# Cross-attention on one Trainium2 core: the weighted rows divided by their sums and the second norm on ScalarE, the weighted rows turned behind the weighting

## Chip, core and metric

The kernel runs on one core of a Trainium2 chip, as one program: TensorE (PE; its weight loads are shown apart, as PEld), VectorE (DVE), ScalarE (ACT), GpSimd (POOL) and SyncE (SP, which issues most of the transfers), each with its own list of instructions, held together by semaphores. The metric is the device time of one execution in microseconds (us). All data are fp32.

## What is computed

Three layers follow each other on 2048 rows (64 latents of 32 batches, 256 wide): a cross-attention to 1601 context rows of each batch, a grouped self-attention, and a mixture of experts. The change lies in the first:

```python
x = x + xattn(layernorm(x), ctx)                  # this change
x = x + attn(layernorm(x))
x = x + moe(layernorm(x))

def xattn(query, ctx):
    q = query @ Wq + bq; k = ctx @ Wk + bk; v = ctx @ Wv + bv
    probs = softmax(einsum('bqd,bkd->bqk', q, k))
    y = einsum('bqk,bkd->bqd', probs, v) + query
    return (y - mean(y)) * rsqrt(var(y) + 1e-5) * gamma + beta
```

The layernorm of its result, which the second layer starts from, is the "second norm" below. It is made in this stage too, and rows and normed rows leave together.

## The kernel before

**The pairs.** A pair is two batches, 128 rows. There are PAIRS = 16. The weights of queries and keys are multiplied beforehand and Wv is applied after the weighting, so that the raw context, in a ring of three slots in SBUF, serves as keys and as values. For pair i the steps are: `blocks_turned` (VectorE transposes the context in 8 column blocks, 5 of them early in a turn and 3 late), `scores` (TensorE, block by block, each behind its `block_ready`), `block_max` and `row_max` (VectorE), `exps` (ScalarE, which also sums), `row_sum` (VectorE, sum and its reciprocal `rinv`), `turn_probs` (TensorE turns the weights in four groups; the last group goes to the unused half of bank U), `turned_out` (ScalarE copies them to SBUF), `weigh` (TensorE, into U, 52 profiled records), `normalise` (U times `rinv` gives `Un`), `flip` (TensorE turns `Un`, in bank M), `UT_evac` (ScalarE copies it), `project` (TensorE, times Wv), `residual` (VectorE: adds the query row, first statistics, `scaled`), `first_norm` (VectorE: writes the new row to `stage[:, 0]`, second statistics), `deviation` (GpSimd: the power -1/2 of a variance), `second_norm` (writes `stage[:, 1]`), and `store` (SyncE sends `stage` to `mid` in DRAM).

**The turns.** The engines run through turns that are written by hand. In turn i TensorE does `scores(i)`, `flip(i-2)`, `weigh(i-1)`, `project(i-2)`, `turn_probs(i)`. VectorE does `block_max(i)`, `row_max(i)`, `second_norm(i-3)`, the 5 early blocks of pair i+1, `normalise(i-1)`, `row_sum(i)`, `residual(i-2)`, the 3 late blocks of pair i+1, `first_norm(i-2)`. ScalarE does `turned_out(i-1)`, `UT_evac(i-2)`, `exps(i)`. Turns 2 to 5 also hold work on queries (on VectorE `x_statistics` and `x_normed` in turn 3, `dots` in turns 2, 4 and 5), and ScalarE issues the stores of queries (`store_q`) behind turns 3 and 5. Turns 6 and up are hardware loops.

**Around the turns.** SyncE's `follow(i)` loads the queries of pair i, stores the rows of pair i-5 once `n1_ready` tells of their second norm, and then issues the ring loads of pair i, part by part behind `pv_done` of pair i-3. `flip` waits for `res_ready`, since it shares bank M with `project`. `first_norm(k)` waits until the rows of pair k-1 have been stored, because there is one `stage`.

**The end.** Behind turn 15 TensorE does `flip(14)`, the first part of `weigh(15)` (16 records), `project(14)`, the rest of `weigh(15)` (36 records), `flip(15)`, `project(15)`, some transposes of weights, and ten filler products (`keep_busy`, L1155), and then turns the first rows of the second layer (L1236), which are read back from `mid`.

## Time and profile before

| | us |
|---|---|
| median of three runs | 538.88 |
| lowest and highest | 538.51, 539.96 |
| the profiled execution, as timed | 540.22 |
| its span, first to last instruction | 538.5 |
| TensorE busy | 498.2 |
| VectorE busy | 399.3 |
| ScalarE busy | 200.1 |
| GpSimd busy | 198.0 |

The profiled execution lasts 1.7 us longer than its span, and 1.3 us longer than the median. Cross-attention takes the first 285 us or so of the span. The times in the rows are microseconds from the start of the span.

### The profile page before, as it was taken

The numbers are of one execution on the slowest core, as the hardware profiler recorded it, in microseconds if no ns is written. First come the engines' busy times: TensorE is split into PE (matmuls) and PEld (weight loads), VectorE is DVE, ScalarE is ACT, GpSimd is POOL, SyncE is SP. The second block draws the span as 40 slices with busy tenths as digits, with TensorE's granted clock in tenths as the row PEclk, the third lists the DMA queues.
The fourth block names the chain that finished last, engine by engine and source line by source line (L and its number), as shares of the span: only waits on it lengthen the run. The fifth ranks groups of instructions, "written<-read, shape, count | busy, mean of one in ns | idle before, by whom it ended". The sixth has DMA issues, their size and how long they took to land.

```text
span 538.5 us, 14453 instructions
## 1 busy us (share of the span) xinstructions
PE 498.2 (93%) x5012; PEld 348.7 (65%) x5013; DVE 399.3 (74%) x1068; ACT 200.1 (37%) x617; POOL 198.0 (37%) x314
## 2 busy tenths in 40 slices
PE   7988899999999999999989999999979899999950
PEld 7765566656666666666655667766735578888840
DVE  3699599999999999999653588888775325555545
ACT  2343323433223333333221366666341035555500
POOL 4000412212221112221222576766766616655620
PEclk9999999999999999999999999999998979999995
DMA  7999688877998888885215999710122245554249
GB/s 276 356 352 243 189 279 291 251 209 252 294 304 286 279 279 272 256 273 196 66 40 165 253 309 297 205 52 2 50 89 90 89 115 157 159 150 120 74 165 302
DMA packets 67348, 108.83 MB, mean 202 GB/s; under 512 B 8115, under 2 KB 49125, under 8 KB 67304
## 3 DMA queue, kind: packets, MB, share of 16 engines
q1 hardware_dynamic: 60888, 97.83, 58.6%
q0 software_dynamic: 3792, 8.43, 4.5%
q10 hardware_dynamic: 2624, 1.97, 1.2%
q8 instruction: 28, 0.46, 0.4%
q14 instruction: 16, 0.13, 0.1%
HBM read 85.31 MB, written 24.85 MB: 205 GB/s over the span
## 4 chain that ended last, share of the span: by engine, by line
PE 70%; DVE 9%; DMA 8%; POOL 5%; issue 4%; ACT 1%; SPq 1%; POOLq 0%; DVEq 0%; ACTq 0%
PE banks L1110 15%; PE banks L1134 15%; PE banks L1516 8%; DMA ring<-in_ctx_dram 5%; POOL rows_by_expert L727 4%; PE banks L1528 4%; PE banks L1122 3%; DVE ctxT L1638 3%; PE banks L1147 3%; PE banks L1069 2%; PE banks L1510 2%; DMA xn_all<-expert_out 2%; PE banks L1243 2%; PE banks L1295 2%; PE banks L1155 2%
## 5 line engine op out<-in xcount | busy, mean ns | idle before, releaser
L1638 DVE STREAM_TRANSPOSE ctxT<-ring 128x832 f32<-128x832 f32 x128 | 121.7, 1009 | 4.2 <-DMA ring<-in_ctx_dram 4.1
L1110 PE MATMUL banks<-ctxT,qT_all 32*64 32x416 f32 (+2 forms) x2048 | 93.9, 498 | 2.5 <-issue 2.1
L1134 PE MATMUL banks<-ring,prob 128*64 128x256 f32 (+1 forms) x832 | 93.6, 381 | 0.7 <-ACT prob L839 0.7
L1134 PEld LDWEIGHTS banks<-ring,prob 128*64 128x64 f32 (+1 forms) x832 | 58.6, 137 | 31.5 <-issue 4.2
L1110 PEld LDWEIGHTS banks<-ctxT,qT_all 32*64 32x64 f32 x2048 | 56.8, 131 | 31.2 <-issue 14.0
L638 POOL TENSOR_TENSOR var<-mv,eps 128x1 f32<-128x1 f32 x32 | 6.3, 196 | 168.6 <-DVE mv L1683 116.5
L761 POOL DMA_INDIRECT expert_out<-prob,dest x47 | 46.2, 984 | 41.6 <-DVE prob L2099 27.7
L852 ACT ACTIVATE prob<-banks,negmax 128x416 f32<-128x416 f32 (+2 forms) x80 | 41.1, 531 | 30.2 <-DVE negmax L1660 30.2
L1516 PE MATMUL banks<-ring,ctxT 128*128 x188 | 50.7, 394 | 0.1
L674 POOL TENSOR_TENSOR ctxT<-ctxT,k_mask 128x1088 f32<-128x1088 f32 x16 | 33.1, 2069 | 25.3 <-ACT ctxT L930 25.3
L839 ACT COPY prob<-banks 128x512 f32<-128x512 f32 x64 | 27.7, 514 | 38.0 <-PE banks L1122 37.9
L2092 DVE TENSOR_TENSOR ctxT<-banks,ctxT 128x128 f32<-128x128 f32 x47 | 13.7, 292 | 36.2 <-ACT ctxT L991 36.2
L1650 DVE TENSOR_REDUCE blockmax<-banks 128x1 f32<-128x416 f32 (+1 forms) x64 | 32.3, 567 | 10.2 <-PE banks L1110 10.2
L1516 PEld LDWEIGHTS banks<-ring,ctxT 128*128 128x128 f32 x188 | 33.3, 197 | 3.4 <-issue 0.5
L856 ACT COPY UT<-banks 128x256 f32<-128x256 f32 x16 | 6.0, 375 | 63.7 <-PE banks L1141 63.7
L1528 PE MATMUL banks<-ring,ctxT 128*128 x94 | 28.0, 381 | 0.0
L1122 PE MATMUL banks<-ident,prob 128*128 128x128 f32 (+1 forms) x208 | 26.1, 274 | 1.7 <-DVE Un L1672 0.9
L1122 PEld LDWEIGHTS banks<-ident,prob 128*128 128x128 f32 (+1 forms) x208 | 23.7, 140 | 4.8 <-ACT w_mem L804 1.6
L2099 DVE TENSOR_SCALAR prob<-banks,share 128x256 f32<-128x256 f32 x47 | 22.6, 481 | 2.7 <-PE banks L1528 0.8
L991 ACT ACTIVATE ctxT<-banks 128x128 f32<-128x128 f32 x47 | 13.0, 278 | 24.0 <-PE banks L1516 24.0
L1510 PE MATMUL banks<-ident,ctxT 128*128 128x128 f32 x94 | 18.9, 286 | 2.9 <-DMA ctxT<-rows_by_expert 2.9
L628 POOL TENSOR_SCALAR x_var<-x_mv 128x4 f32<-128x4 f32 (+1 forms) x5 | 1.3, 258 | 53.6 <-DVE x_mv L1587 53.6
(269 smaller groups left out, 940.5 us busy)
## 6 DMA issues: line engine op xcount, KB each, us to landing
ring<-in_ctx_dram SPq DMA_DIRECT2D x48, 1024.0 KB
qT_all<-q_by_pair SPq DMA_DIRECT2D x56, 128.0 KB, 8.9
rows_by_expert<-blank SPq DMA_DIRECT2D x8, 774.0 KB, 7.2
ctxT<-rows_by_expert SPq DMA_DIRECT2D x47, 129.0 KB, 2.1
mid<-stage SPq DMA_DIRECT2D x31, 128.0 KB, 2.3
ring<-in_ctx_dram SPq DMA_DIRECT2D x16, 130.0 KB
ctxT<-mid SPq DMA_DIRECT2D x16, 128.0 KB, 4.5
qT_all<-mid SPq DMA_DIRECT2D x16, 128.0 KB, 4.9
```

The costliest lines, as they stand in the source:

```text
L674: pool.tensor_tensor(k_blk, k_T.unsqueeze(2).broadcast_to([P, GB, HEADS, NP]), k_mask[:, :].unsqueeze(1).unsqueeze(3).broadcast_to([P, GB, ...
L761: pool.indirect_dma_start(y_dram, bass.IndirectOffsetOnAxis(ap=dest[:, s:s + 1], axis=0), y_sb[:, r, :], None, bounds_check=TOPK * TOK - 1 ...
L839: act.copy(probT[0:rows, ks[0]:ks[-1] + 1, :].rearrange("p a b -> p (a b)"), PT_BANKS[g][0:rows, 0:len(ks) * P]).then_inc(probT_copied, 1)
L852: act.activation(to, of, ACT.Exp, bias=negmax[:, 0:1], accum_out=sums[:, n:n + 1]).then_inc(exp_done, 1)
L1110: last = pe.matmul(S[a][64 * b:64 * b + 64, 0:KW[a]], q_rep[mine, r, c, 64 * b:64 * b + 64], ctxT[mine, c, b, 0:KW[a]], start=c == 0, stop ...
L1122: last = pe.transpose(PT_BANKS[g][0:rows, a * P:a * P + P], prob[:, k * P:k * P + rows], ident[:, :])
L1134: last = pe.matmul(U[64 * b:64 * b + 64, 0:D], probT[0:rows, k, 64 * b:64 * b + 64], ring[0:rows, r, b, k, :], start=k == 0, stop=k == KT)
L1510: last = pe.transpose(bank[r % 2][:, dh * P:dh * P + P], row_in[:, r, dh * P:dh * P + P], ident[:, :])
L1516: last = pe.matmul(bank[2 + p][:, 0:2 * HID], rowT[:, p, k, :], w_gu[:, bass.ds(e, 1), k, :].squeeze(1), start=k == 0, stop=k == DH - 1)
L1528: pe.matmul(bank[6 + p][:, 0:D], hidT[:, p, :], w_down[:, bass.ds(e, 1), :].squeeze(1), start=True, stop=True)\
L1638: dve.transpose(ctxT[:, c].rearrange("p b (k j) -> p (b k) j", j=Q), ring[:, r].rearrange("p b k c -> p (b k) c")[:, :, columns(c):columns ...
L1650: dve.tensor_reduce(blockmax[:, a:a + 1], S[a][:, 0:KW[a]], AX.X, ALU.max).then_inc(blockmax_ready, 1)
```

## The change

`normalise` moves from VectorE to ScalarE, behind `exps(i)`, as an activation with a scale of each row; since there is one `Un`, it now waits until `flip` of the pair before is through (`UT_done`), and VectorE's reciprocal waits until the last `normalise` has read `rinv`. `second_norm(i-3)` moves to ScalarE too, ahead of `exps(i)`, as scale and bias; the bias, minus mean times deviation, is made by GpSimd with two more instructions in `deviation(k, 1)`. The second norm of the last pair stays on VectorE. `UT_evac` goes behind `exps` and `normalise`. On TensorE `flip(i-2)` goes behind `weigh(i-1)`, and `project(i-2)` behind `turn_probs(i)`. The lines behind turn 15 on TensorE are not edited.

```diff
@@ -636,8 +636,15 @@
 
                 pool.wait_ge(mv_ready, 2 * k + (n + 1))
                 pool.tensor_tensor(var[:, n:n + 1], mv[:, n, 1:2], eps[:, :], ALU.add).then_inc(var_ready, 1)
-                pool.wait_ge(var_ready, 2 * k + (n + 1))
-                pool.tensor_tensor(rstd[:, n:n + 1], var[:, n:n + 1], m_half[:, 0:1], ALU.pow).then_inc(rstd_ready, 1)
+                if n == 0:
+                    pool.wait_ge(var_ready, 4 * k + 1)
+                    pool.tensor_tensor(rstd[:, 0:1], var[:, 0:1], m_half[:, 0:1], ALU.pow).then_inc(rstd_ready, 1)
+                else:
+                    pool.tensor_tensor(nmean[:, 1:2], mv[:, 1, 0:1], minus[:, :], ALU.mult).then_inc(var_ready, 1)
+                    pool.wait_ge(var_ready, 4 * k + 3)
+                    pool.tensor_tensor(rstd[:, 1:2], var[:, 1:2], m_half[:, 0:1], ALU.pow).then_inc(var_ready, 1)
+                    pool.wait_ge(var_ready, 4 * k + 4)
+                    pool.tensor_tensor(nmr[:, 1:2], nmean[:, 1:2], rstd[:, 1:2], ALU.mult).then_inc(rstd_ready, 1)
 
             def add_vectors(i):
 
@@ -851,11 +858,26 @@
                         to, of = by_slab[:, lo // Q, a, 0:hi - lo], S[a][:, lo:hi]
                     act.activation(to, of, ACT.Exp, bias=negmax[:, 0:1], accum_out=sums[:, n:n + 1]).then_inc(exp_done, 1)
 
+            def normalise(k, first=False):
+
+                act.wait_ge(pv_done, (k + 1) * len(KPARTS))
+                act.wait_ge(rinv_ready, k + 1)
+                if not first:
+                    act.wait_ge(UT_done, k)
+                act.activation(Un[:, :], U[:, 0:D], ACT.Copy, scale=rinv[:, 0:1]).then_inc(Un_ready, 1)
+
+            def second_norm(k):
+
+                act.wait_ge(rstd_ready, 2 * k + 2)
+                act.activation(stage[:, 1, :].rearrange("p (h v) -> p v h", h=HEADS),
+                               stage[:, 0, :].rearrange("p (v h) -> p v h", h=HEADS), ACT.Identity, bias=nmr[:, 1:2],
+                               scale=rstd[:, 1:2]).then_inc(n1_ready, 1)
+
             def UT_evac(i):
                 act.wait_ge(UT_done, i + 1)
                 act.copy(UT[:, :, :].rearrange("p a b -> p (a b)"), M[:, 0:D]).then_inc(UT_copied, 1)
 
-            def turn(i, ahead=True, back1=True, back2=True, rows=None, queries=None):
+            def turn(i, ahead=True, back1=True, back2=True, back3=True, rows=None, queries=None):
 
                 if back1:
                     turned_out(i - 1)
@@ -863,19 +885,25 @@
                     rows_turned(rows)
                 if queries:
                     query_blocks(queries)
+                if back3:
+                    second_norm(i - 3)
+                if ahead:
+                    exps(i)
+                    normalise(i - 1)
                 if back2:
                     UT_evac(i - 2)
-                if ahead:
-                    exps(i)
+                if back1 and not ahead:
+                    normalise(i - 1)
 
             exps(0)
             query_blocks(0)
             turned_out(0)
             exps(1)
+            normalise(0, first=True)
             rows_turned(1)
             query_blocks(1)
             store_q(1)
-            turn(2, rows=2)
+            turn(2, back3=False, rows=2)
             turn(3, queries=2)
             store_q(2)
             turn(4, rows=3)
@@ -1165,21 +1193,21 @@
                     queries_turned(rows)
                 if queries:
                     queries_of(queries)
+                if back1:
+                    pe.wait_ge(Un_ready, i - 1)
+                    weigh(i - 1, (r - 1) % RING)
                 if back2:
                     if back3:
                         pe.wait_ge(res_ready, i - 2)
                     flip(i - 2)
-                if back1:
-                    pe.wait_ge(Un_ready, i - 1)
-                    weigh(i - 1, (r - 1) % RING)
-                if back2:
-                    project(i - 2)
                 if rows:
                     pe.wait_ge(xnT_copied, 2 * rows + 4)
                 if queries:
                     pe.wait_ge(qT_copied, 2 * queries + 2)
                 if ahead:
                     turn_probs(i)
+                if back2:
+                    project(i - 2)
 
             pe.wait_ge(bk_row_copied, 1)
             scores(0, 0, 0, True)
@@ -1659,17 +1687,13 @@
                 dve.wait_ge(topped_ready, i + 1)
                 dve.tensor_tensor(negmax[:, :], shift[:, bass.ds(i, 1)], topped[:, :], ALU.subtract).then_inc(negmax_ready, 1)
 
-            def row_sum(k):
+            def row_sum(k, first=False):
                 dve.wait_ge(exp_done, (k + 1) * len(EXPS))
                 dve.tensor_reduce(rowsum[:, :], sums[:, :], AX.X, ALU.add).then_inc(rowsum_ready, 1)
                 dve.wait_ge(rowsum_ready, k + 1)
+                if not first:
+                    dve.wait_ge(Un_ready, k)
                 dve.reciprocal(rinv[:, :], rowsum[:, :]).then_inc(rinv_ready, 1)
-
-            def normalise(k):
-
-                dve.wait_ge(pv_done, (k + 1) * len(KPARTS))
-                dve.wait_ge(rinv_ready, k + 1)
-                dve.tensor_scalar(Un[:, :], U[:, 0:D], rinv[:, 0:1], None, ALU.mult).then_inc(Un_ready, 1)
 
             def residual(k):
 
@@ -1712,22 +1736,18 @@
                                              scalar=bk_row[:, D:D + 1], op0=ALU.mult, op1=ALU.add,
                                              accum_out=shift[:, a:a + 1]).then_inc(dot_ready, 1)
 
-            def turn(i, r, round_, ahead=True, more=True, back1=True, back2=True, back3=True, also=(), of_x=None):
+            def turn(i, r, round_, ahead=True, more=True, back2=True, also=(), of_x=None):
 
 
                 if ahead:
                     block_max(i)
                     row_max(i)
-                if back3:
-                    second_norm(i - 3)
                 if more:
                     blocks_turned(i + 1, (r + 1) % RING, round_ + (1 if r == RING - 1 else 0), range(0, EARLY))
                 if also:
                     dots(*also)
                 if of_x:
                     x_statistics(of_x)
-                if back1:
-                    normalise(i - 1)
                 if ahead:
                     row_sum(i)
                 if back2:
@@ -1750,13 +1770,12 @@
             blocks_turned(1, 1, 0, range(BLOCKS))
             dots(1, 3)
             x_statistics(2)
-            row_sum(0)
+            row_sum(0, first=True)
 
             block_max(1)
             row_max(1)
             x_normed(2)
             blocks_turned(2, 2, 0, range(EARLY))
-            normalise(0)
             row_sum(1)
             blocks_turned(2, 2, 0, range(EARLY, BLOCKS))
             dots(3, 4)
@@ -1764,7 +1783,7 @@
             x_normed(3)
 
             dve.wait_ge(rest_loaded, 112)
-            turn(2, 2, 0, back3=False, also=(4, 6))
+            turn(2, 2, 0, also=(4, 6))
             turn(3, 0, 1, of_x=4)
             turn(4, 1, 1, also=(6, 9))
             turn(5, 2, 1, also=(9, PAIRS))
@@ -1772,11 +1791,8 @@
                 for u in range(RING):
                     turn(it * RING + u, u, it)
             turn(PAIRS - 1, (PAIRS - 1) % RING, PAIRS // RING, more=False)
-            second_norm(PAIRS - 3)
             residual(PAIRS - 2)
             first_norm(PAIRS - 2)
-            normalise(PAIRS - 1)
-            second_norm(PAIRS - 2)
             dve.wait_ge(prep_loaded, 16 * (GB + 6))
             dve.tensor_copy(w_qp[:, :].rearrange("p (h v) -> p h v", h=HEADS), w_q.rearrange("p (v h) -> p h v", h=HEADS))\
                 .then_inc(w_qp_ready, 1)
```

TensorE in a turn of the loop, before; `Un` is what `flip` turns, `prob` what `turn_probs` turns, `UT` and `wv` are `project`, `ring` is `weigh`:

```order
L1110 MATMUL banks<-ctxT,qT_all 64x384 x2
L1141 MATMUL banks<-ident,Un 128x128 [waits Un_ready,res_ready]
L1141 MATMUL banks<-ident,Un 128x128
L1127 REGISTER_ALU [waits Un_ready]
L1134 MATMUL banks<-ring,prob 64x256 [waits probT_copied]
L1134 MATMUL banks<-ring,prob 64x256 x25
L1147 MATMUL banks<-wv,UT 128x256 [waits UT_copied]
L1147 MATMUL banks<-wv,UT 128x256
L1116 ISA
L1122 MATMUL banks<-ident,prob 128x128 [waits exp_done]
L1122 MATMUL banks<-ident,prob 128x128 x11
L1122 MATMUL banks<-ident,prob 65x128 [waits Un_ready]
```

The same place now:

```order
L1138 MATMUL banks<-ctxT,qT_all 64x384 x2
L1155 REGISTER_ALU [waits Un_ready]
L1162 MATMUL banks<-ring,prob 64x256 [waits probT_copied]
L1162 MATMUL banks<-ring,prob 64x256 x25
L1169 MATMUL banks<-ident,Un 128x128 [waits Un_ready,res_ready]
L1169 MATMUL banks<-ident,Un 128x128
L1144 ISA
L1150 MATMUL banks<-ident,prob 128x128 [waits exp_done]
L1150 MATMUL banks<-ident,prob 128x128 x11
L1150 MATMUL banks<-ident,prob 65x128 [waits Un_ready]
L1175 MATMUL banks<-wv,UT 128x256 [waits UT_copied]
L1175 MATMUL banks<-wv,UT 128x256
```

The two turns of `Un` stand behind the weighting, and the projection behind the turned weights, as the last thing ahead of the next scores.

ScalarE at the end of cross-attention (the copies of the last turned weights, then `UT_evac(14)` and `UT_evac(15)` in one row, then copies of turned weights of later layers), before:

```order
L839 COPY prob<-banks 128x512 [waits probT_done] x3
L839 COPY prob<-banks 65x128 [waits probT_done]
L856 COPY UT<-banks 128x256 [waits UT_done] x2
L890 COPY turned<-banks 128x512 [waits prep_done] x4
L892 DMA mid<-stage 64x512 [waits n1_ready]
```

The same place now:

```order
L846 COPY prob<-banks 128x512 [waits probT_done] x3
L846 COPY prob<-banks 65x128 [waits probT_done]
L872 ACTIVATE stage<-stage,nmr,rstd 128x16x16 [waits rstd_ready]
L878 COPY UT<-banks 128x256 [waits UT_done]
L867 ACTIVATE Un<-banks,rinv 128x256 [waits UT_done,rinv_ready,pv_done]
L872 ACTIVATE stage<-stage,nmr,rstd 128x16x16 [waits rstd_ready]
L878 COPY UT<-banks 128x256 [waits UT_done]
L918 COPY turned<-banks 128x512 [waits prep_done] x4
```

Each `UT_evac` now stands behind a second norm: that of pair 14 behind the norm of pair 13, that of pair 15 behind the norm of pair 14.

TensorE at the end, now (before, L1147 for pair 13 stood ahead of L1122, and the rest was the same):

```order
L1150 MATMUL banks<-ident,prob 65x128 [waits Un_ready]
L1175 MATMUL banks<-wv,UT 128x256 [waits UT_copied]
L1175 MATMUL banks<-wv,UT 128x256
L1169 MATMUL banks<-ident,Un 128x128 [waits Un_ready,res_ready]
L1169 MATMUL banks<-ident,Un 128x128
L1162 MATMUL banks<-ring,prob 64x256 [waits probT_copied,Un_ready]
L1162 MATMUL banks<-ring,prob 64x256 x7
L1175 MATMUL banks<-wv,UT 128x256 [waits UT_copied]
```

`project(13)` now stands right ahead of `flip(14)`, which waits for the `residual` that reads it; the last row, `project(14)`, has the other 18 instructions of `weigh(15)` queued behind it.

## Rows read from the trace of the kernel before

**Rows 1.** The page: busy us, share of the span, instructions, by engine.

```profile
PE 498.2 (93%) x5012; PEld 348.7 (65%) x5013; DVE 399.3 (74%) x1068; ACT 200.1 (37%) x617; POOL 198.0 (37%) x314
```

**Rows 2.** Timeline of TensorE in turn 10: start, length, line, names [idle before <-releaser].

```profile
188.39 5.83 PE L1134 MATMUL banks<-ring,prob 128*64 128x256 f32 x52
194.15 1.13 PE L1147 MATMUL banks<-wv,UT 128*128 128x256 f32 x4
195.12 1.58 PE L1122 MATMUL banks<-ident,prob 128*128 128x128 f32 x13
196.63 5.82 PE L1110 MATMUL banks<-ctxT,qT_all 32*64 32x416 f32 x128
202.38 0.44 PE L1141 MATMUL banks<-ident,Un 128*128 128x128 f32 x2
202.74 0.44 PE L1134 MATMUL banks<-ring,prob 128*64 128x256 f32 x2
```

**Rows 3.** Timeline of VectorE in the same turn.

```profile
190.82 0.51 DVE L1703 TENSOR_SCALAR stage<-stage,mv,rstd 128x256 f32<-128x256 f32 x1
...
196.58 0.43 DVE L1678 TENSOR_TENSOR res<-banks,xn_all 128x256 f32<-128x256 f32 x1
...
198.21 2.88 DVE L1638 STREAM_TRANSPOSE ctxT<-ring 128x832 f32<-128x832 f32 x3
...
202.58 0.59 DVE L1650 TENSOR_REDUCE blockmax<-banks 128x1 f32<-128x416 f32 x1 [0.39 <-PE banks L1110]
```

**Rows 4.** Timeline of weight loads: the last block of the scores of pair 10.

```profile
186.91 0.46 PEld L1110 LDWEIGHTS banks<-ctxT,qT_all 32*64 32x64 f32 x16 [0.24 <-DVE ctxT L1638]
```

**Rows 5.** Waits from 60 to 285 us: us in total, times, longest.

```profile
PEld banks L1122 <- DVE Un L1672: 1.6, 3, 0.7
```

**Rows 6.** Timelines of VectorE and of weight loads in turn 3.

```profile
88.50 0.42 DVE L1678 TENSOR_TENSOR res<-banks,xn_all 128x256 f32<-128x256 f32 x1 [0.30 <-PE banks L1147]
...
91.39 2.89 DVE L1638 STREAM_TRANSPOSE ctxT<-ring 128x832 f32<-128x832 f32 x3
...
94.37 0.21 PEld L1110 LDWEIGHTS banks<-ctxT,qT_all 32*64 32x64 f32 x12 [0.17 <-issue]
```

**Rows 7.** Timeline of all engines behind turn 15.

```profile
267.84 0.42 DVE L1678 TENSOR_TENSOR res<-banks,xn_all 128x256 f32<-128x256 f32 x1 [0.30 <-PE banks L1147]
...
270.14 1.95 PE L1134 MATMUL banks<-ring,prob 128*64 128x256 f32 x16 [0.69 <-ACT prob L839]
...
272.02 1.13 PE L1147 MATMUL banks<-wv,UT 128*128 128x256 f32 x4
272.22 0.50 DVE L1703 TENSOR_SCALAR stage<-stage,mv,rstd 128x256 f32<-128x256 f32 x1 [0.93 <-POOL rstd L640]
...
278.31 0.37 ACT L856 COPY UT<-banks 128x256 f32<-128x256 f32 x1 [8.04 <-PE banks L1141]
...
278.73 1.13 PE L1147 MATMUL banks<-wv,UT 128*128 128x256 f32 x4 [0.46 <-ACT UT L856]
```

**Rows 8.** Timeline of GpSimd in the second layer: first and last of the four-step deviation.

```profile
311.47 0.19 POOL L687 TENSOR_TENSOR var<-mv,eps 128x1 f32<-128x1 f32 x1
...
312.52 0.19 POOL L692 TENSOR_TENSOR nmr<-nmean,rstd 128x1 f32<-128x1 f32 x1
```

**Rows 9.** A ScalarE line with scale and bias: duration in ns (min/median/max), first and last start.

```profile
L903 ACT ACTIVATE ctxT<-x_all,nmr,rstd x12: 588/600/602, 312.7 to 374.3; 128x256 f32<-128x256 f32 x6, 128x256 f32 x6
```

**Rows 10.** Timelines of TensorE: its first work behind two long idle times of later layers.

```profile
403.00 1.20 PE L1410 MATMUL banks<-ring,turned 128*128 128x512 f32 x2 [2.05 <-DVE ctxT L2012]
...
432.00 1.09 PE L1510 MATMUL banks<-ident,ctxT 128*128 128x128 f32 x4 [2.94 <-DMA ctxT<-rows_by_expert]
```

**Rows 11.** Windows: busy share (count) of PE, PEld, DVE, ACT, POOL; granted clock, DMA, GB/s.

```profile
404.00:405.00 1.00, 1.00 (x3) 0.48 (x2) 0.00 (x0) 0.23 (x1) 0.78 (x1) 0.50 0.00 0
...
407.00:408.00 1.00, 1.00 (x3) 0.38 (x2) 0.00 (x0) 0.00 (x0) 0.73 (x1) 0.83 0.37 132
...
432.00:433.00 1.00, 1.00 (x4) 0.64 (x4) 0.32 (x4) 0.30 (x1) 0.00 (x0) 0.50 0.80 231
```

## The prediction, made before the changed kernel was run

> **What bounds the kernel now.** I read the page first: TensorE is busy for 498.2 us, 93% of the span, VectorE for 74%, ScalarE for 37% [rows 1]. Then a turn of the loop on TensorE [rows 2]. From start to start, the weighting takes 194.15 - 188.39 = 5.76 us, the projection 0.97, the turned weights 196.63 - 195.12 = 1.51, the scores 5.75, the flip 0.36. The sum, 14.35, is the whole turn (202.74 - 188.39): TensorE stands still nowhere. VectorE is nearly as full: it waits 0.39 us for the last scores [rows 3], and its last late block comes so late that the weight load of the eighth block of scores waited 0.24 us for it [rows 4]; TensorE's products themselves did not stop. So what the change takes off VectorE can only pay where TensorE waits for VectorE. That is one row of the waits: 1.6 us in 3 places, where the last group of turned weights waited for `Un` [rows 5].
>
> **Work taken away and added, in a turn.** VectorE loses the second norm (0.51 us, [rows 3]) and the division, which I take at the same size. ScalarE gets both. The nearest row has scale and bias and takes 0.60 us [rows 9]; a plain copy of the same size takes 0.37 [rows 7]. I take 0.6 for the norm, 0.5 for the division. ScalarE is idle for over half of the time [rows 1]; the norm stands where it would wait for the maxima, and the division where it would wait for the end of the weighting, so I cost both at nothing in the loop: the weighting's 5.76 us and the turned weights' 1.51 hide them. If that cover went, it would be 1.1 us a turn.
>
> The Trainium skill speaks against this move: "ScalarE: Activation LUTs", Rules for kernel authors, wants adds and multiplies on VectorE. What ACT_TABLE_LOAD costs, on the same page, gives 186 ns plus 0.833 ns per element plus 93 ns for each operand of a row, by estimate 0.59 us for the norm; the 0.60 of this trace agrees [rows 9]. By it the sum below stays as it is.
>
> **The removed waits: -1.6 us.** The division now runs right behind the weighting and the flip: flip, 0.4 for its landing, 0.5, while 12 of the 13 groups of turned weights (1.4 us) are still ahead of the one that waits. So the three waits go [rows 5]. Their bounds are 0 and 1.6; I take 1.6.
>
> **The later projection: +0.6 us in the loop, +1.5 us in turn 3.** The projection moves behind the turned weights, so it starts 1.51 us later in the turn. VectorE's `residual` reads it and stands ahead of the three late blocks. In the loop the projection would start at 195.66 and end, at 1.13 us, at 196.79; the residual started at 196.58 and now can't before 196.83, 0.25 us later. So VectorE's saved 1 us turns into waiting for TensorE, and the late blocks end 0.25 us later than before. The last weight load had no slack [rows 4]: it moves by about 0.2 us. What reaches TensorE lies between 0 (the loads run ahead of the products, and the flip between two other kinds of turning may shed some of its 0.36) and 0.2. I take 0.07 for each of nine turns (5 to 15, without the two behind a loop's end), 0.6 us; the bounds are 0 and 1.8.
>
> In turn 3 VectorE does more, and the residual already waited 0.30 us for the projection [rows 6]. Everything behind it is a chain: residual at 88.50, late blocks from 91.39 to 94.28, and the eighth block's weight load at 94.37, directly behind [rows 6]. The projection 1.51 us later moves all of it: +1.5. VectorE's saving ahead of the residual doesn't help, because the residual waits. ScalarE's `store_q` behind turns 3 and 5 now queues behind the late `UT_evac`, and `turned_out` behind that; in turn 3 the same 1.5 us cover it, in turn 5 it may cost a few tenths, which I leave to the range.
>
> **The end: +3.2 us.** This is the largest term. Here `project(13)` is behind the turned weights of pair 15, and there are no scores to cover anything.
> - `residual(13)` started at 267.84 [rows 7]; it moves by the turned weights less their overlap, 1.4 us, to 269.3.
> - From it to the end of GpSimd's deviation took 272.22 - 267.84 = 4.38 us [rows 7]. GpSimd now does two more small steps: the four take 312.71 - 311.47 = 1.24 us [rows 8], 0.4 over the two. So the second norm of pair 13 can start at 274.1 and takes 0.6 on ScalarE.
> - `UT_evac(14)` stands behind it. It starts at 274.6, and the projection followed such a copy by 278.73 - 278.31 = 0.42 us [rows 7]: `project(14)` at 275.0. Before, it was at 272.02 [rows 7]. That is +3.0 us. Behind it wait the 36 remaining records of `weigh(15)`, and all that follows.
> - `UT_evac(15)` stands behind the second norm of pair 14 in the same way. Residual at 275.0 + 1.2, then 4.4 + 0.4 + 0.6, gives 281.5 for the copy and 281.9 for `project(15)`, against 278.73 [rows 7]: +3.2 us in all. The fillers and the next layer stand behind it on TensorE, and the rows of pair 15 leave even later, so nothing takes it back. The bounds are 2.4 (norm at 0.37, no extra steps) and 4.
>
> **The clock: +1.3 us.** Between the first part of `weigh(15)` and `project(14)` TensorE now idles for 275.0 - 272.0 = 3 us. The trace has two idle times of 2 us or more ahead of product work: 2.05 and 2.94 us [rows 10]. Behind both the granted clock was 0.50, the 1.2 GHz level; the first time from 404 into the window from 407, over 3 us [rows 11]. Work at half rate for 3.3 us loses 1.7 us; part of it may fall into idle time. I take 1.3, with 0 and 3.3 (twice as long) as the bounds.
>
> **Sum.** -1.6 + 0.6 + 1.5 + 3.2 + 1.3 = +5.0 us. On the profiled execution, 540.2, that is 545.2. It lay 1.3 us above the median of the three runs, so the median should be 538.9 + 5.0 = **543.9 us**.
>
> **Rivals.**
> - The clock holds: the same without the last term, 538.9 + 3.7 = 542.6. For it: one place, with transposes and products on both sides; the two cases of the trace are few.
> - VectorE is the true bound of the loop, and the kernel gets faster. For it: the weight load that waited [rows 4], and 1 us less work a turn. If each of the 13 turns gave back only 0.7 us, that is -9.1; with the end, 538.9 - 9.1 + 4.5 = 534.3. It decides if the projection, once TensorE's turn shrinks, comes earlier than VectorE asks for it. Against it: the pieces of TensorE's turn fill it without a gap [rows 2]; no order of them is shorter.
> - The end doesn't stall: if `UT_evac(14)` finds the norm of pair 13 finished, the change does in sum +0.5, 539.4. For that the chain of 4.4 us behind the residual would have to hide behind a first part of `weigh(15)` of 1.9 us [rows 7]. It can't, unless later layers absorb the delay.
> - The transfers are late: the stores of queries go out 6 us later, and the load of pair 8 queues behind them; +1.5 more, 545.4. The second norm is earlier on ScalarE by a microsecond, and that helps the loads, since SyncE stores rows ahead of them.
>
> **How the numbers follow.** Forecast (clock falls) 0.45, clock holds 0.30, late transfers 0.09, faster 0.06, no stall 0.10. The first three lie between 541.2 (-1.6 + 0 + 1.5 + 2.4 + 0: no loss in the loop, the short end, the clock held) and 546.3 (-1.6 + 1.8 + 1.5 + 4 + 1.7). That holds 8 in 10, so the range is 541.2 to 546.3. A measurement can tell about 0.3%, 1.6 us, from no change: slower means above 540.5. Slower 0.84, the same 0.10, faster 0.06.
>
> **What would show it.** The turn in the loop stays between 14.35 and 14.6 us on TensorE, and VectorE waits for `project` ahead of each residual. The last turned group waits for `Un` nowhere. The scores of pair 4 end 1.5 us later. Behind turn 15 TensorE idles for 3 us ahead of `project(14)`, released by the copy of `UT`, which waited for the norm; and the windows behind it show a clock of 0.50, or not. I am wrong if the turn is shorter than 14.2 us, if that idle time is under 1 us, or if the second layer starts less than 2 us later.

## The result, and the profile after

| us | before | changed |
|---|---|---|
| median of 20 executions each, taken in turns | 539.46 | 541.14 |
| lowest and highest | 537.08, 542.31 | 537.60, 543.99 |
| the profiled execution, as timed | 540.22 | 541.16 |
| its span | 538.5 | 539.4 |

The changed kernel is slower: the ratio of the medians is 1.0046, with a 95% interval of 1.0031 to 1.0061, some 2.5 us. A second series on another occasion (below) gave 1.0057 [1.0035, 1.0079]. The forecast was +5.0 us and 543.9. The sign was right and the size twice too large: on the median that the forecast started from, the ratio gives 538.88 x 1.0046 = 541.4, just inside the low end of the range (541.2). The plain median, 541.14, lies just under it.

The page of the changed kernel, busy time by engine:

```profile
PE 497.0 (92%) x5012; PEld 344.0 (64%) x5013; DVE 391.6 (73%) x1037; ACT 216.7 (40%) x648; POOL 203.4 (38%) x346
```

Beside [rows 1], VectorE lost 7.7 us and ScalarE gained 16.6. The two steps were 14.9 us of VectorE's records; part of the difference is one small step, `topped`, which grew by 3.7 us in sum (below). The groups (line, operation, names and shapes, count; busy us and mean ns; idle time before them, and what ended it) show what the two moved steps cost. First VectorE before, the second norm and the division:

```profile
L1703 DVE TENSOR_SCALAR stage<-stage,mv,rstd 128x256 f32<-128x256 f32 x16 | 8.1, 505 | 2.0 <-POOL rstd L640 2.0
...
L1672 DVE TENSOR_SCALAR Un<-banks,rinv 128x256 f32<-128x256 f32 x15 | 6.9, 458 | 3.7 <-PE banks L1134 3.7
```

Then ScalarE in the changed kernel, the norm and the division:

```profile
L872 ACT ACTIVATE stage<-stage,nmr,rstd 128x256 f32<-128x256 f32 x15 | 12.4, 823 | 74.5 <-POOL nmr L647 74.5
L867 ACT ACTIVATE Un<-banks,rinv 128x256 f32<-128x256 f32 x15 | 7.1, 475 | 17.0 <-PE banks L1169 11.7 <-PE banks L1162 5.3
```

The division costs the same on both, 0.46 and 0.48 us. The norm takes 0.82 us instead of 0.51, and not the 0.6 that I read off [rows 9]. The idle time ahead of it, 74.5 us, stands ahead of `exps` and `UT_evac` too, since all are in one list.

**A turn of the loop.** Turn i is counted from the start of the scores of pair i to the start of those of pair i+1. Timeline of TensorE at the end of turn 11 and the start of turn 12 of the changed kernel (start, length, line, names); L1162 is the weighting, L1169 the flip, L1150 the turned weights, L1175 the projection, L1138 the scores:

```profile
207.23 0.44 PE L1169 MATMUL banks<-ident,Un 128*128 128x128 f32 x2
207.57 1.64 PE L1150 MATMUL banks<-ident,prob 128*128 128x128 f32 x13
209.04 1.03 PE L1175 MATMUL banks<-wv,UT 128*128 128x256 f32 x4
210.00 5.82 PE L1138 MATMUL banks<-ctxT,qT_all 32*64 32x416 f32 x128
215.75 5.83 PE L1162 MATMUL banks<-ring,prob 128*64 128x256 f32 x52
```

Against [rows 2] the flip takes 0.34 from start to start (before 0.36), the turned weights 1.47 (1.51), the projection 0.96 (0.97). Turn 11 is 14.28 us, against the 14.35 of [rows 2]. The nine turns from the start of the scores of pair 6 to that of pair 15 took 254.80 - 123.66 = 131.14 us before, and take 252.88 - 124.59 = 128.29 now: **2.85 us less**. The forecast had 1.0 less for the whole loop.

The last block of scores did become later, as forecast. Timeline of the weight loads of the same scores (those of pair 11, which start at 195.72):

```profile
200.60 0.24 PEld L1138 LDWEIGHTS banks<-ctxT,qT_all 32*64 32x64 f32 x16 [0.49 <-DVE ctxT L1666]
201.46 1.49 PEld L1162 LDWEIGHTS banks<-ring,prob 128*64 128x64 f32 x16 [0.62 <-issue]
```

Its first load stands 4.88 us behind the start of the scores; in turn 6, where it did not wait, it stands at 4.48. The first product of the block slips too, from 4.61 to 4.92. And yet the weighting's first load comes at 5.74, as it does anyway (from 196.63 to 202.38 in [rows 2], the flip there, it was 5.75): the slip is gone before the block ends. What is next is another chain. In turn 12 the last of `exps` ends at 221.80, and the turned weights start at 221.85. In turns 9 to 14 they follow `exps` by 0.05 us, so the maxima on VectorE and the exponentials on ScalarE now set these turns.

Part of that chain is new. Timelines of GpSimd and VectorE, in turn 10 before and in turn 11 of the changed kernel; `topped` is a step of `row_max`, `x_all` one of GpSimd's own additions:

```profile
189.50 0.73 POOL L647 TENSOR_TENSOR x_all<-x_all,beta_b 128x256 f32 x1
190.55 0.16 DVE L1658 TENSOR_TENSOR topped<-rowmax,shift 128x1 f32<-128x1 f32 x1
```

```profile
203.89 0.73 POOL L654 TENSOR_TENSOR x_all<-x_all,beta_b 128x256 f32 x1
204.00 0.63 DVE L1686 TENSOR_TENSOR topped<-rowmax,shift 128x1 f32<-128x1 f32 x1
```

Before, and in e4 below, every `topped` takes 0.16 us. In the changed kernel GpSimd's addition comes later and runs when `topped` starts in turns 4, 5 and 7 to 15, and each of these ends 0.01 to 0.02 us behind the addition, after 0.22 to 0.72 us. In turns 6 to 8, where `exps` still ends by 11.65 us into the turn, the turn is 14.17 us; in turns 9 to 14 `exps` ends at 11.80 to 11.84, and the turn is 14.28 to 14.32. That `topped` waits for GpSimd is read off these ends; no run moves the addition alone.

**Turns 3 and 5.** Both became longer, 18.33 us (17.84 before) and 18.59 (17.97). At the end of turn 5 TensorE shows a wait that was not there, and one of 0.46 us at the end of turn 3. TensorE and ScalarE (ACTq is its issuing of transfers, L820 is `store_q`):

```profile
121.75 0.33 ACTq L820 DMA_DIRECT2D q_by_pair<-w_mem  x1
122.07 0.36 ACT L878 COPY UT<-banks 128x256 f32<-128x256 f32 x1
122.11 1.43 ACTq L820 DMA_DIRECT2D q_by_pair<-w_mem  x3
123.75 1.72 ACT L846 COPY prob<-banks 128x512 f32<-128x512 f32 x4 [1.31 <-PE banks L1150]
...
124.59 2.84 PE L1138 MATMUL banks<-ctxT,qT_all 32*64 32x416 f32 x60 [0.72 <-ACT prob L846]
```

`turned_out` (L846) empties the banks that the next scores write. It queues behind four stores, 1.8 us of issuing. Before, the four were issued from 115.89 on, while `exps` still ran.

**The end.** Timeline of TensorE and ScalarE behind turn 15, which answers to [rows 7]:

```profile
268.12 1.95 PE L1162 MATMUL banks<-ring,prob 128*64 128x256 f32 x16
...
272.04 0.81 ACT L872 ACTIVATE stage<-stage,nmr,rstd 128x256 f32<-128x256 f32 x1 [4.74 <-POOL nmr L647]
272.67 0.40 ACT L878 COPY UT<-banks 128x256 f32<-128x256 f32 x1
273.12 1.13 PE L1175 MATMUL banks<-wv,UT 128*128 128x256 f32 x4 [3.05 <-ACT UT L878]
274.18 4.11 PE L1162 MATMUL banks<-ring,prob 128*64 128x256 f32 x36
...
280.18 1.13 PE L1175 MATMUL banks<-wv,UT 128*128 128x256 f32 x4 [0.81 <-ACT UT L878]
...
292.38 0.38 PE L1264 MATMUL banks<-ident,ctxT 128*128 128x128 f32 x2
```

This is what the prediction described: 3.05 us of idle TensorE ahead of `project(14)`, released by the copy of `UT`, which stood behind the norm, which waited for GpSimd. From the end of the scores of pair 15 to `project(15)` it was 278.73 - 260.61 = 18.12 us, and it is 280.18 - 258.70 = 21.48: **+3.36 us** (forecast +3.2).

In these two profiles the granted clock stayed at 1.00 through the end. Windows of the changed kernel (busy us with counts of PE, PEld, DVE, ACT, POOL; then the granted clock, DMA share, GB/s):

```profile
270.00:272.00 2.00, 0.07 (x2) 0.00 (x0) 0.66 (x3) 0.00 (x0) 1.07 (x4) 1.00 0.00 0
272.00:274.00 2.00, 0.89 (x4) 0.68 (x4) 0.00 (x0) 1.03 (x2) 0.00 (x1) 1.00 0.02 5
```

**The account.** Between the ends of the scores of pairs 2 and 15 the changed kernel needs 1.92 us less (196.14 against 198.06), from there to the first row of the second layer (L1264) 3.36 more (33.68 against 30.32). In sum the second layer starts 1.4 us later (292.38 against 290.94). The span ends 0.9 us later, since what is left of it took 247.0 us instead of 247.6. In that part the lead of 0.8 us comes between 416 and 445 us, where the granted clock was at 0.50 for 6.8 us in the profile before (from 431.2) and for 3.4 us in this one (from 435.5); the change has no instruction there.

### The profile page after: what moved, and what is told of

Its sections match the earlier page's. It is cut to its first block, busy times and chain, and to the rows that moved or that the text cites. A ratio compares the mean times of both kernels' runs of the same rounds, so it can differ in the third digit from the quotient of the medians.

```text
span 539.4 us, 14541 instructions
## 1 busy us (share of the span) xinstructions
PE 497.0 (92%) x5012; PEld 344.0 (64%) x5013; DVE 391.6 (73%) x1037; ACT 216.7 (40%) x648; POOL 203.4 (38%) x346
## 3 DMA queue, kind: packets, MB, share of 16 engines
q10 hardware_dynamic: 2624, 1.97, 1.1%
## 4 chain that ended last, share of the span: by engine, by line
PE 52%; issue 20%; POOL 10%; DVE 7%; DMA 6%; ACT 1%; SPq 1%; POOLq 1%; ACTq 0%; DVEq 0%
PE banks L1544 8%; PE banks L1138 8%; PE banks L1162 7%; POOL rows_by_expert L734 4%; PE banks L1556 4%; PE banks L1097 3%; DMA ring<-in_ctx_dram 2%; PE banks L1538 2%; DVE ctxT L1666 2%; DMA xn_all<-expert_out 2%; PE banks L1271 2%; PE banks L1150 2%; PE banks L1323 2%; PE banks L1183 2%; PE banks L1278 2%
## 5 line engine op out<-in xcount | busy, mean ns | idle before, releaser
L1138 PE MATMUL banks<-ctxT,qT_all 32*64 32x416 f32 (+2 forms) x2048 | 93.6, 500 | 2.2 <-ACT prob L846 1.2
L1162 PE MATMUL banks<-ring,prob 128*64 128x256 f32 (+1 forms) x832 | 93.6, 381 | 0.0
L1162 PEld LDWEIGHTS banks<-ring,prob 128*64 128x64 f32 (+1 forms) x832 | 58.3, 137 | 36.8 <-issue 9.3
L1138 PEld LDWEIGHTS banks<-ctxT,qT_all 32*64 32x64 f32 x2048 | 53.2, 131 | 36.6 <-DVE ctxT L1666 10.7
L872 ACT ACTIVATE stage<-stage,nmr,rstd 128x256 f32<-128x256 f32 x15 | 12.4, 823 | 74.5 <-POOL nmr L647 74.5
L846 ACT COPY prob<-banks 128x512 f32<-128x512 f32 x64 | 27.5, 525 | 6.1 <-PE banks L1150 6.1
L1150 PE MATMUL banks<-ident,prob 128*128 128x128 f32 (+1 forms) x208 | 25.8, 275 | 0.8 <-ACT w_mem L811 0.8
L1150 PEld LDWEIGHTS banks<-ident,prob 128*128 128x128 f32 (+1 forms) x208 | 22.7, 140 | 2.6 <-ACT w_mem L811 1.6
```

The source lines that it names most:

```text
L846: act.copy(probT[0:rows, ks[0]:ks[-1] + 1, :].rearrange("p a b -> p (a b)"), PT_BANKS[g][0:rows, 0:len(ks) * P]).then_inc(probT_copied, 1)
L1138: last = pe.matmul(S[a][64 * b:64 * b + 64, 0:KW[a]], q_rep[mine, r, c, 64 * b:64 * b + 64], ctxT[mine, c, b, 0:KW[a]], start=c == 0, stop ...
L1150: last = pe.transpose(PT_BANKS[g][0:rows, a * P:a * P + P], prob[:, k * P:k * P + rows], ident[:, :])
L1162: last = pe.matmul(U[64 * b:64 * b + 64, 0:D], probT[0:rows, k, 64 * b:64 * b + 64], ring[0:rows, r, b, k, :], start=k == 0, stop=k == KT)
```

## The experiments

Each was timed in turns with the kernel before (medians of 538.96 to 539.46 in the four series), and its ratio is to that. The counts are small: 20 executions of the changed kernel, 12 each of e1 to e4, 8 of e10, 7 of the changed kernel again, 6 each of e7 and e9, 4 of e6 and 2 of e5. The columns behind the ratio are from one profile each. "Loop" is the time from the end of the scores of pair 2 to the end of those of pair 15, "end" from there to `project(15)`, "second layer" from there to the first turned row of the second layer:

| kernel | median, us | ratio, interval | loop | end | second layer |
|---|---|---|---|---|---|
| before | 539.46 | 1 | 198.06 | 18.12 | 30.32 |
| changed | 541.14 | 1.0046 [1.0031, 1.0061] | 196.14 | 21.48 | 33.68 |
| changed again | 542.64 | 1.0057 [1.0035, 1.0079] | 196.15 | 22.79 | 35.00 |
| e1 ScalarE's end in another order | 539.94 | 1.0014 [0.9990, 1.0038] | 196.20 | 18.04 | 32.15 |
| e2 e1, and stores earlier | 538.60 | 0.9993 [0.9977, 1.0010] | 195.33 | 18.05 | 32.22 |
| e3 late blocks first | 541.76 | 1.0035 [1.0006, 1.0064] | 196.32 | 23.90 | 36.11 |
| e4 ScalarE's part alone | 538.20 | 0.9986 [0.9969, 1.0004] | 196.21 | 18.11 | 30.81 |
| e5 TensorE's part alone | 554.03 | 1.0271 [1.0254, 1.0289] | 207.86 | 18.97 | 34.07 |
| e6 six fillers | 544.87 | 1.0104 [1.0087, 1.0121] | 196.15 | 23.55 | 38.89 |
| e7 both orders mixed | 536.16 | 0.9946 [0.9932, 0.9961] | 194.33 | 18.13 | 30.70 |
| e9 three fillers | 544.43 | 1.0098 [1.0065, 1.0130] | 196.18 | 21.52 | 36.85 |
| e10 old order in turn 15 | 541.52 | 1.0052 [1.0030, 1.0074] | 196.70 | 20.18 | 35.51 |

**e1: is the end one queue?** The changed kernel, with ScalarE's last steps in another order:

```diff
-            turn(PAIRS, ahead=False)
-            turn(PAIRS + 1, ahead=False, back1=False)
+            turned_out(PAIRS - 1)
+            UT_evac(PAIRS - 2)
+            second_norm(PAIRS - 3)
+            normalise(PAIRS - 1)
+            UT_evac(PAIRS - 1)
+            second_norm(PAIRS - 2)
```

> The changed kernel with one edit behind turn 15 on ScalarE: the copy of the turned rows of pair 14 goes ahead of the second norm of pair 13, and that of pair 15 ahead of the norm of pair 14. Theory (the end costs what the change loses, the loop gains): from the end of the scores of pair 15 to project(15) 21.5 us become 18.1 to 18.3, TensorE's idle time of 3 us ahead of project(14) is gone, the whole is 3.3 us shorter than the changed kernel and about 1.9 us shorter than the kernel before (0.9965). Rival (the loss lies elsewhere, say in the clock or in later layers, and the end is hidden by what follows): the end gets shorter and the whole stays within 1 us of the changed kernel, at 1.004 of the kernel before.

The end fell from 21.48 to 18.04 us: without the copies behind the norms the whole +3.36 is gone. But the second layer won only 1.5 us of it, and the time missed its expectation of 0.9965: the ratio is 1.0014, and its interval takes in 1. Timelines of VectorE and TensorE in this kernel (L1721 is `first_norm`):

```profile
274.25 0.48 DVE L1721 SCALAR_TENSOR_TENSOR stage<-scaled,rstd,x_all 128x256 f32<-128x256 f32 x1 [3.00 <-DMA mid<-stage]
...
289.19 0.41 PE L1268 MATMUL banks<-ident,ctxT 128*128 128x128 f32 x2 [1.74 <-DMA qT_all<-mid]
```

Now the one `stage` is next: `first_norm` waits 3 us for the store of the pair before (0.84 us in the kernel before), and the second layer's first rows arrive 1.74 us after TensorE is ready for them. That is a new wait behind the removed one.

**e2: do the stores hold turns 3 and 5?** e1, and `store_q` right behind `exps` in these turns:

```diff
                 if ahead:
                     exps(i)
+                    if send:
+                        store_q(send)
                     normalise(i - 1)
...
-            turn(3, queries=2)
-            store_q(2)
+            turn(3, queries=2, send=2)
             turn(4, rows=3)
-            turn(5, queries=3)
-            store_q(3)
+            turn(5, queries=3, send=3)
```

> As e1_end, and ScalarE issues the stores of queries of turns 3 and 5 between the exponentials and the division, instead of behind the copy of the turned rows. Theory (the four issues, 1.8 us, hold up the copy of the turned weights that the next scores wait for): TensorE's wait of 0.7 us ahead of the scores of pair 6 goes, turn 5 is 17.8 us instead of 18.6 from scores to scores; the scores of pair 4 start 0.5 us earlier and still end where they did, since VectorE's late blocks end them. 0.8 us less than e1_end. Rival (the copy waits for TensorE, not for the issues): turn 5 stays at 18.6.

Turn 5 went from 18.66 us in e1 to 17.80, and `turned_out` now starts with no idle time ahead of it:

```profile
121.51 1.72 ACT L846 COPY prob<-banks 128x512 f32<-128x512 f32 x4
```

Turn 3 shrank by 0.67 us, 18.47 to 17.80, and turn 4 gave it all back, 15.59 to 16.26. There the late blocks are behind the late `residual`. Weight loads of e2 in turn 4:

```profile
93.03 0.24 PEld L1142 LDWEIGHTS banks<-ctxT,qT_all 32*64 32x64 f32 x16 [1.12 <-DVE ctxT L1670]
93.95 0.24 PEld L1142 LDWEIGHTS banks<-ctxT,qT_all 32*64 32x64 f32 x16 [0.69 <-DVE ctxT L1670]
```

So in turn 3 the two delays ran beside each other, and in turn 5 the stores were the only one. In all the edit is worth 0.87 us.

**e3: does the late block matter in the loop?** The changed kernel, with VectorE's late blocks ahead of `residual`:

```diff
                 if ahead:
                     row_sum(i)
+                if more:
+                    blocks_turned(i + 1, ...)
                 if back2:
                     residual(i - 2)
                 if of_x:
                     x_normed(of_x)
-                if more:
-                    blocks_turned(i + 1, ...)
```

> The changed kernel with VectorE's three late blocks ahead of the residual instead of behind it, so that the late projection no longer moves them. Theory A (a late last block of up to 0.3 us costs TensorE nothing in the loop, it costs only in turn 3): the turn in the loop stays 14.17 to 14.32 us although the blocks come a microsecond earlier, and the scores of pair 4 end 1 us earlier. Theory B (the late blocks bound the turn, 14.3 us is VectorE's): the turn falls to 14.17 or less in every turn, 1 us or more over the loop beside turn 3. Against both: the first norm may come later, as it loses the cover for GpSimd's 0.9 us, and block_max with it; then the turn grows.

The first load of the last block now stood at 4.48 us in every turn. Turn 7, in which it had stood at 4.89 in the changed kernel, took 14.17 us in both. The late last block costs nothing there. Turn 4 took 15.19 instead of 15.74: there the late blocks do cost 0.55. From pair 8 to pair 15, though, the loop was 0.73 us longer (100.69 against 99.96). VectorE in this kernel:

```profile
199.00 0.48 DVE L1717 SCALAR_TENSOR_TENSOR stage<-scaled,rstd,x_all 128x256 f32<-128x256 f32 x1 [0.69 <-POOL rstd L641]
```

The late blocks used to cover GpSimd's deviation; without that cover `first_norm` waits 0.69 us for it, and VectorE, not TensorE, sets some of the turns. In the end the granted clock was 0.50 for 6.8 us from 270.7 on. That is within the 3.05 us of idle time (268.5 to 271.6) ahead of `project(14)`:

```profile
271.59 2.07 PE L1175 MATMUL banks<-wv,UT 128*128 128x256 f32 x4 [3.05 <-ACT UT L878]
```

The same four records took 1.13 us in the changed kernel's own profile, and the end 23.90 us instead of 21.48. Thus the fall that was forecast exists; it is not there in every profile.

**e4: ScalarE's part alone.** Division and second norm on ScalarE, TensorE in the order of before, ScalarE's end as in e1:

```diff
                 if back2:
                     flip(i - 2)
                 if back1:
                     weigh(i - 1, (r - 1) % RING)
+                if back2:
+                    project(i - 2)
                 if ahead:
                     turn_probs(i)
-                if back2:
-                    project(i - 2)
```

> ScalarE's part alone: division and second norm on ScalarE, TensorE in the order of before (flip, weighting, projection, turned weights), the copy of the turned rows ahead of the exponentials, and the end as in e1_end. Theory A (the 0.4 us at each end of TensorE's loop shows only because the last turned group waits for a late division just ahead of it): the last group waits nowhere, and the loop's end costs nothing: the turns of pairs 8 and 11 are 14.4 us instead of 14.8 and 15.0. Theory B (it is hidden only where the projection stands last): those turns stay at 14.7 to 14.8. For the other turns both expect 14.36 as before; if the 0.07 to 0.19 us by which the changed kernel's turns are shorter are due to TensorE's order they are absent here.

All nine turns of the loop took 14.36 to 14.37 us, against 131.14 / 9 = 14.57 on average before. The wait for `Un` is gone, and something else with it. Before, turns 7, 8 and 11 were long: 15.05, 14.76, 15.03. TensorE before, in turns 7, 8 and 11 (L1122 the turned weights, L1110 the scores; "issue" is idle time with no releaser that the profile shows):

```profile
152.81 0.32 PE L1122 MATMUL banks<-ident,prob 128*65 128x128 f32 x1 [0.43 <-DVE Un L1672]
...
167.88 5.82 PE L1110 MATMUL banks<-ctxT,qT_all 32*64 32x416 f32 x128 [0.34 <-ACT prob L839]
...
211.66 2.82 PE L1110 MATMUL banks<-ctxT,qT_all 32*64 32x416 f32 x57 [0.39 <-issue]
```

Turns 8, 11 and 14 end a pass of the hardware loop over three ring slots. Two of the three showed 0.34 to 0.39 us ahead of the next scores, and neither the changed kernel nor e4 shows it in any. My reading is that TensorE's list gets to the branch late when its last instruction, the group that needs `Un`, is held up or nearly so; with `Un` early, the branch lies beside the products that are still running. That fits e4 and is not proved by it. Two things in the trace count against it: the profile puts the 0.34 us down to the copy of turned weights, and `Un` was written at the same place, 13.55 to 14.0 us into the turn, in turns 8, 10, 13 and 14, of which only turn 8 shows the idle time. Turn 14 leaves the loop and does not jump back, so the jump itself is another reading. Against 14.40, the three turns lost 0.65 + 0.36 + 0.63 = 1.64 us.

The wait in turn 7 has a cause further up: VectorE waited 0.53 us for the ring load of pair 8 (at 147.64), and `Un` was late behind it. In e4 VectorE waited 0.54 us at the same place, and turn 7 is 14.36 all the same. A third wait for `Un` stood in turn 4, ahead of these nine. There e4 took 15.23 us against 15.88 before, 0.65 less.

**e5: TensorE's part alone.** The kernel before, with TensorE's new order and `UT_evac` behind `exps`, division and norm still on VectorE:

```diff
+                if back1:
+                    weigh(i - 1, (r - 1) % RING)
                 if back2:
                     flip(i - 2)
-                if back1:
-                    weigh(i - 1, (r - 1) % RING)
-                if back2:
-                    project(i - 2)
                 if ahead:
                     turn_probs(i)
+                if back2:
+                    project(i - 2)
...
             def normalise(k, first=False):

                 dve.wait_ge(pv_done, (k + 1) * len(KPARTS))
                 dve.wait_ge(rinv_ready, k + 1)
+                if not first:
+                    dve.wait_ge(UT_done, k)
```

> TensorE's part alone: flip behind the weighting, projection behind the turned weights, the copy of the turned rows behind the exponentials, while division and second norm stay on VectorE as before. Theory (the order of TensorE needs the division on ScalarE, since VectorE reaches it only 1.6 us after the weighting ends, behind its five early blocks): TensorE waits for Un ahead of the last turned group in every turn, by some 0.5 to 1 us, and the turn in the loop is 14.8 to 15.5 us; 6 to 12 us slower than before. Rival (VectorE has room; only the order counts): the turns are 14.2 to 14.3 as in the changed kernel.

It is 2.7% slower (two executions), with a wait in twelve turns. The rows of the waits (us in total, times, longest) and one turn of TensorE:

```profile
PE banks L1122 <- DVE Un L1674: 10.4, 12, 1.3
```

```profile
137.48 1.47 PE L1122 MATMUL banks<-ident,prob 128*128 128x128 f32 x12
139.79 0.32 PE L1122 MATMUL banks<-ident,prob 128*65 128x128 f32 x1 [0.84 <-DVE Un L1674]
```

The loop took 207.86 - 198.06 = 9.8 us more, and these waits are 10.4. The new order of TensorE makes `Un` urgent, since the flip must be through before the division may write it; only an engine that is free then can follow. The two halves of the change are not independent.

**e6: fillers in the idle time.** To see if the idle time makes the clock fall, six filler products ahead of `project(14)` in the changed kernel:

```diff
             weigh(PAIRS - 1, (PAIRS - 1) % RING, KPARTS[0:1])
+            keep_busy(6)
             project(PAIRS - 2)
```

> The changed kernel with six products that nobody reads (2.6 us) in TensorE's idle time ahead of project(14). Theory C (in part of the executions the clock falls in that idle time, as it did in the profile of e3_late_first, where it took 2.4 us): the granted clock is never 0.50 between 268 and 280 us, and over many executions the mean time is 0.5 to 1.5 us below that of e8_changed_again, with less spread. Rival (the clock does not matter there): the same within 0.5 us. By the trace alone, from the end of the scores of pair 15 to project(15): 21.5 us in both.

It came out slower than either expectation, and part of that is a mistake in sizing. Timeline of TensorE:

```profile
267.84 5.42 PE L1183 MATMUL banks<-w_mem,ident 128*128 128x512 f32 x12
273.09 1.03 PE L1175 MATMUL banks<-wv,UT 128*128 128x256 f32 x4
```

Each filler is two records of 0.44 us; six of them fill 5.4 us, where 3.05 were idle, and `project(14)` came 2.2 us later behind the scores than in the changed kernel.

**e9: three fillers.**

```diff
             weigh(PAIRS - 1, (PAIRS - 1) % RING, KPARTS[0:1])
+            keep_busy(3)
             project(PAIRS - 2)
```

> The changed kernel with 3 filler products (6 records of 0.44 us, 2.7 us) instead of 6 in the idle time ahead of project(14). Six of them ran for 5.42 us, where the idle time was 3.05: project(14) came 2.1 us late, and the granted clock fell all the same, later, at 281.1. Theory A (the loss of the six was their length, and a fall of the clock depends on more than this one idle time): project(14) starts within 0.2 us of where it does without fillers, 15.0 us behind the end of the scores of pair 15; the end up to project(15) takes 21.4 to 21.7 us unless the clock falls in it; the median is that of the changed kernel, a ratio of 1.003 to 1.006 to the kernel before. Theory B (the idle time is what makes the clock fall in the end, and filling it keeps the clock): the same start of project(14), no window at 0.50 between 268 and 292 us, and 1 to 1.5 us less than the changed kernel in the median, a ratio of 1.000 to 1.003.

Now they fit: 0.28 us of idle time is left, `project(14)` starts 14.46 us behind the scores (14.42 without fillers; the 15.0 of the expectation was wrong), and the end takes 21.52 us, as without them. Still the median is 544.43, above both bounds. In the profile the clock fell all the same, only later, and for longer. TensorE, then windows:

```profile
268.26 2.84 PE L1183 MATMUL banks<-w_mem,ident 128*128 128x512 f32 x6
271.39 1.13 PE L1175 MATMUL banks<-wv,UT 128*128 128x256 f32 x4 [0.28 <-ACT UT L878]
...
278.45 1.80 PE L1175 MATMUL banks<-wv,UT 128*128 128x256 f32 x4 [0.82 <-ACT UT L878]
...
281.33 3.67 PE L1256 MATMUL banks<-ident,ring 128*128 128x128 f32 x16
```

```profile
276.00:278.00 2.00, 0.96 (x8) 0.30 (x4) 0.24 (x1) 1.11 (x3) 1.11 (x4) 1.00 0.00 0
278.00:280.00 2.00, 1.55 (x4) 1.19 (x5) 0.00 (x0) 0.39 (x2) 0.00 (x0) 0.69 0.31 71
280.00:282.00 2.00, 2.00 (x9) 1.31 (x8) 1.60 (x5) 0.00 (x0) 0.39 (x2) 0.50 0.26 60
```

The sixteen transposes of L1256 took 3.67 us; in the changed kernel's profile they took 1.97. The theory that the 3 us of idle time are what the clock falls on, and that filling them saves it, does not hold in this profile, and the median did not drop. The fall starts at 278.8. One of the same 6.8 us is also in the profiles of e5 (from 287.8), e6 (281.1) and e10 (277.6), each near the two waits of 0.67 to 1.73 and 0.46 to 0.82 us around `flip(15)`. But the kernel before, e1, e2, e4 and e7 have waits of 0.67 to 0.68 and 0.46 us there and kept the clock through them (in e1 it fell later, at 290.7, behind the 1.74 us wait). The changed kernel's profile has 0.67 and 0.81, almost as e9, and kept it too. What decides it stays open. Nor is the clock the whole of e9's loss: its profile loses 3.2 us up to the second layer and 2.8 more behind it, and the mean clock of its six executions, 0.978, is no lower than that of the changed kernel's 20, 0.977. Where the rest goes was not traced.

**e8: the changed kernel again**, with no edit:

> The changed kernel as it is, on the same chip as the others. All theories: 1.002 to 1.006 of the kernel before. If the clock falls in its end in this profile, project(15) is 23 to 24 us behind the scores of pair 15; if it does not, 21.5 us.

This profile has the fall. TensorE, then a window:

```profile
272.18 1.88 PE L1175 MATMUL banks<-wv,UT 128*128 128x256 f32 x4 [3.05 <-ACT UT L878]
```

```profile
272.00:274.00 2.00, 1.82 (x5) 1.00 (x6) 0.00 (x0) 0.13 (x1) 0.00 (x0) 0.60 0.44 102
```

Same program, same idle time of 3.05 us, and the clock went to 0.50, the 1.2 GHz level, for 3.4 us (from 272.4). The end is 22.79 us instead of 21.48, so the fall costs 1.31 us; 1.3 was the term of the forecast. Over the executions time and clock go together. In the 20 of the first series the time goes down by 5.0 us for each 0.01 that the mean granted clock of the execution goes up: the fastest (537.6) had 0.984, the three slowest (543.91 to 543.99) 0.973 to 0.976. That is a figure of this kernel alone: in the 35 executions of the kernel before in the series of e1 it is 2.0 us. In this series the mean clock was 0.9751 for the changed kernel and 0.9805 for the one before.

**e10: how the end divides.** The changed kernel with the old order in turn 15 alone, its end unchanged:

```diff
-            turn(PAIRS - 1, (PAIRS - 1) % RING, (PAIRS - 1) // RING)
+            turn(PAIRS - 1, (PAIRS - 1) % RING, (PAIRS - 1) // RING, old=True)
...
+                if old:
+                    pe.wait_ge(res_ready, i - 2)
+                    flip(i - 2)
                 if back1:
                     pe.wait_ge(Un_ready, i - 1)
                     weigh(i - 1, (r - 1) % RING)
-                if back2:
+                if back2 and not old:
...
+                if old:
+                    project(i - 2)
```

> The changed kernel with the old order in turn 15 alone (TensorE: flip, weigh, project, turn_probs; ScalarE: UT_evac ahead of the norm and the exps), and its end as the change left it (each UT_evac behind a second norm). It splits the 3.36 us that the end became longer. Theory A (two parts: the chain from residual(13) starts 1.4 us later, and GpSimd's steps and the norm lengthen it by 1.4 to 1.9 us): the chain starts 1.4 us earlier again, the idle time ahead of project(14) falls from 3.05 to 1.6 us, project(15) starts 20.0 us behind the end of the scores of pair 15 (18.12 before, 21.48 changed), and the ratio is 1.001 to 1.003. Theory B (the place of project(13) costs nothing, since everything waits for UT_evac(14) behind the norm, whose own inputs are ready earlier than I think): no change, 21.4 us, ratio 1.004 to 1.006.

TensorE at the same place:

```profile
270.15 1.13 PE L1179 MATMUL banks<-wv,UT 128*128 128x256 f32 x4 [1.61 <-ACT UT L878]
```

The idle time fell from 3.05 to 1.61 us and the end from 21.48 to 20.18: 1.3 us of the 3.36 come from the later `project(13)`, the other 2.1 from the norms ahead of the copies. Both count only while the copies stand behind the norms: e1 moves the copies alone and has the whole back. The time missed its expectation (1.0052, where 1.001 to 1.003 was expected). In this profile the clock was at 0.50 for 6.8 us from 277.6 on, and the second layer started 35.51 us behind the scores. Also VectorE waited 1.14 us for the ring load of pair 8, and turn 8 took 14.69 us instead of 14.16.

**e7: a version that beats both.** e2, with the old order in turns 3 and 15 on TensorE and ScalarE (the switch `old` of e10, also in turn 3):

```diff
-            turn(3, 0, 1, queries=2)
+            turn(3, 0, 1, queries=2, old=True)
...
-            turn(3, queries=2, send=2)
+            turn(3, queries=2, send=2, old=True)
...
-            with act.Fori(6, PAIRS) as i:
+            with act.Fori(6, PAIRS - 1) as i:
                 turn(i)
+            turn(PAIRS - 1, old=True)
```

> e2_end_store, with the order of before on TensorE and ScalarE (flip, weighting, projection, turned weights; the copy of the turned rows ahead of the exponentials) in turns 3 and 15 alone. Theory: in turn 3 the projection is read 1.4 us sooner, VectorE's late blocks no longer hold the scores of pair 4, and turn 4 (scores to scores) is 15.2 us instead of 16.3; behind turn 15 each store of rows, which the next first norm waits for, starts 1.4 us sooner, and from the end of the scores of pair 15 to the first product of the second layer it is 30.8 us instead of 32.2. The stretch from the end of the scores of pair 2 to there is 225.1 us, against 228.4 before, 229.8 changed and 227.6 in e2_end_store: 3 us faster than before (0.994). Rival (what the end gives is lost in later layers): within 1 us of the kernel before.

536.16 us, 0.9946 [0.9932, 0.9961]. Turns 3 to 5 take 17.84, 15.19 and 17.80, the loop is 3.73 us shorter than before, and the end is the old one:

```profile
266.74 1.13 PE L1183 MATMUL banks<-wv,UT 128*128 128x256 f32 x4
...
273.44 1.13 PE L1183 MATMUL banks<-wv,UT 128*128 128x256 f32 x4 [0.46 <-ACT UT L878]
...
286.01 0.41 PE L1278 MATMUL banks<-ident,ctxT 128*128 128x128 f32 x2 [0.20 <-DMA qT_all<-mid]
```

`project(14)` follows the weighting with no gap, and the rows arrive nearly in time. Against e2, the old order in turns 3 and 15 gives 1.0 us in the loop (195.33 to 194.33) and 1.5 at the start of the second layer (32.22 to 30.70).

## Why the forecast had the sign and missed the size

**The removed waits, -1.6: too small, by a term that was missed.** The three waits of [rows 5] are 0.67 us in turn 4, 0.67 in turn 7 and 0.23 in turn 11, and they are gone. e4 prices what went: 0.65 us in turn 4, and 1.64 in turns 7, 8 and 11, of which the waits are about half (0.65 + 0.23). The rest showed at the ends of a loop pass, which the prediction had not seen as a cost. Together that is 2.3 us and not 1.6.

**The later projection in the loop, +0.6: wrong, and the step that failed most.** The chain was right up to the weight load: VectorE waits for the projection (L1702 by L1175, 0.44 us in turn 11), the late blocks are later, the last block's load too. "The last weight load had no slack" was the false sentence. The load had no slack against the block, but the stream of products had slack against the load: the load slipped by 0.40 us (4.48 to 4.88), and the block's end did not move. e3 shows it in turn 7: the load back at 4.48, the turn at 14.17 all the same. The remark that the flip might shed some of its 0.36 was put beside the sum instead of into it. Pieces of 0.34 and 1.47, in three turns of 0.28 and 1.42, made each of the nine turns (131.14 - 1.64 - 128.29) / 9 = 0.13 us shorter on average, -1.2 us, even though `topped` behind GpSimd's addition took back some 0.1 us in six of them. Between +0.6 and -1.2 lie 1.8 us of the 2.5 by which the forecast was too high.

**Turn 3, +1.5: +0.49 in turn 3, -0.14 in turn 4.** The late blocks moved by 92.76 - 91.39 = 1.37 us [rows 6], as said, and the last load stands 5.44 us into the scores. But the loads of these blocks had slack as well. The scores of pair 4 end 96.60 - 95.62 = 0.98 us later, against the 1.5 that were expected. The +0.49 in turn 3 itself is the stores. With these out of the way the late projection costs turn 4 16.26 - 15.19 = 1.07 us (e2 against e7); in the changed kernel it hides behind the stores' delay and the 0.65 us that the wait for `Un` in turn 4 gave back.

**The stores, left to the range: +0.6 in turn 5.** The mechanism was named and given no number. It had one: four issues, 1.8 us, ahead of `turned_out`, and TensorE waited 0.72 us for it.

**The end, +3.2: right.** +3.36, by the steps as they were written. Two sizes inside were off: the norm is 0.82 us and not 0.6, and the chain starts a little earlier. The Trainium skill ("ScalarE: Activation LUTs", What ACT_TABLE_LOAD costs) gave by estimate 0.59 us for the norm; the rows show 0.82, so the measurement decides. It reads and writes in groups of 16 by 16, unlike the row it was taken from; no run sets that apart. The rule of the Trainium skill on the same page (Rules for kernel authors), to keep adds and multiplies on VectorE, is given there for bf16. In this fp32 kernel it holds on the price (0.82 us for 0.51, the division 0.48 for 0.46), and yet the move pays in the loop: the loop of e4 is 1.85 us shorter than before, and its time is not slower.

**The clock, +1.3: right in size where it comes, and it does not always come.** One profile of the changed kernel lacks the fall, the other has it at 1.31 us; in what share of the executions it comes is not shown. The reason given, "idle for 3 us, so the clock falls", was too strong: the same 3.05 us had it in two profiles (e8, e3) and not in a third, and fillers did not help. The upper end of the range also took 1.7 us for this term, where its own bound was 3.3; with it the range would have ended at 547.9.

**The sum.** By the profile with a quiet clock: -1.9 in the loop, +3.4 in the end, +1.4 at the start of the second layer. With the fall +2.8. The measured ratio, +2.5 us, lies between them, nearer to the second. That it fell inside the range at all is partly luck: the terms that were too high (the loop's order by 1.8 us, the waits by 0.7, turn 3 by 0.5) were offset in part by the stores of turn 5 (0.6), which stood in no term.

**The rivals.** "VectorE is the true bound" is out: the turn gained 0.13 us where it would have gained 0.7. "The end doesn't stall" is out. "The transfers are late" did not show in the changed kernel's profiles. It showed in e10, where the ring load of pair 8 cost turn 8 0.5 us, and in e1, in another form, when the wait for the norms was taken away. "The clock holds" is what the first profile shows, and not the second. Two of the three signs of "I am wrong if" came true. Three turns were at 14.17 us, under the 14.2 that it named, and that was the sign of the missed term. And in the first profile the second layer starts 1.4 us later, less than the 2 that it named; in the second it is 2.8.

## What to carry over

Moving a step to a freer engine is costed by its place in that engine's list, not by its length: here the loop hid 1.3 us a turn on ScalarE, and the same order with nothing to cover it, in the last two turns, cost 3.4 us, more than the loop had won. An order that is right for the loop need not be right for its last turns, and giving the last turns, and turn 3, orders of their own and moving the stores (e7) turned the loss into a gain. A late weight load is not a late end of its block: a slip of 0.4 us was absorbed, and a slip counts only from where the stream of products itself stops.

## What the runs showed that I had not expected

- A branch at the end of a pass of TensorE's loop shows as 0.34 to 0.39 us of idle time in two passes of the kernel before, and not at all once `Un` is early (e4, nine turns of 14.36 us). That the late instruction is what exposes it is argued from these patterns, with no run for the branch alone, and turns 8 and 14, alike in `Un`, differ.
- A step of one element a row on VectorE, `topped`, takes 0.16 us alone and up to 0.72 us when an addition on GpSimd is running at its start, and then ends 0.01 to 0.02 us behind it. The change shifted the two onto each other, and `exps` and some turns moved with it.
- The same program had the granted clock at 1.00 throughout the end in one execution and at 0.50 for 3.4 us in another, a difference of 1.31 us. Some executions of other kernels had it for 6.8 us. A single profile does not tell what the clock costs in the median; for that the clocks of many executions have to be set beside their times.
- Filling 2.8 of 3.05 idle microseconds with products (e9) did not keep the clock: it fell 7 us later than in e8 and for twice as long. The median rose by 2 to 3 us over the changed kernel, not all of it by the clock. What the clock follows there is open.
- A second norm on ScalarE, from one half of `stage` to the other in groups of 16 by 16, takes 0.82 us, where a scale and bias on plain rows takes 0.60 [rows 9].
